# A two-layer graph network: a shorter bank count in the layer-0 sums, deviations by chunks in the first stage, one-hots three windows ahead in the one-head sums

## What is computed

```python
xn = _layernorm(x)
x = x + gnn0(xn, edges) + mix0(xn)       # 8 heads of 32, edge features in the score
x = x + ffn0(_layernorm(x))              # 8 experts
xn = _layernorm(x)
x = x + gnn1(xn, edges) + mix1(xn)       # 4 heads of 128, then 1 head of 256
x = x + ffn1(_layernorm(x))              # 32 experts

# in each graph step, per head:
ex    = jnp.exp(alpha - segment_max(alpha, dst)[dst])
attn  = ex / segment_sum(ex, dst)[dst]
out   = segment_sum(h[src] * attn[..., None], dst)
```

## Time and profile before

| | us |
|---|---|
| three runs | 3051.1, 3053.57, 3061.77 |
| median | 3053.57 |
| the profiled execution | 3050.74 |
| its span, first to last instruction | 3049.0 |
| PE busy | 2105.7 (69%) |
| DVE busy | 2085.5 (68%) |
| POOL busy | 1440.7 (47%) |
| ACT busy | 827.2 (27%) |

### The profile page before, as it was taken

The page is one execution under the profiler, slowest core; times in us unless marked ns, Lnnn a source line. Parts: engine busy times, 40 slices in busy tenths (PEclk is TensorE's granted clock), DMA queues, the critical chain, the costliest instruction groups (busy, mean ns, idle before and its releaser), DMA issues. The chain is left out here.

```text
span 3049.0 us, 51563 instructions
## 1 busy us (share of the span) xinstructions
PE 2105.7 (69%) x11892; PEld 1580.5 (52%) x11893; DVE 2085.5 (68%) x4524; ACT 827.2 (27%) x2459; POOL 1440.7 (47%) x1486
## 2 busy tenths in 40 slices
PE   2634878757887389948665499999756188887372
PEld 2322434445665355624565377787645177776252
DVE  7496888888888343353478688888677277778442
ACT  2314444431001212124200467676500000001110
POOL 2477777700000310130553777777357677771234
PEclk9866998979998599979777699999856599998586
DMA  4777999935775278843997788898589645550085
GB/s 151 208 205 218 269 269 270 271 139 172 229 232 149 98 256 271 271 125 118 340 393 263 238 278 281 277 287 275 137 285 269 190 130 158 159 148 20 35 257 175
DMA packets 447837, 649.13 MB, mean 213 GB/s; under 512 B 67552, under 2 KB 328286, under 8 KB 447123
## 3 DMA queue, kind: packets, MB, share of 16 engines
q1 hardware_dynamic: 329747, 351.62, 37.0%
q0 software_dynamic: 82640, 248.85, 27.6%
q10 hardware_dynamic: 35296, 46.90, 4.5%
HBM read 478.83 MB, written 169.68 MB: 213 GB/s over the span
## 5 line engine op out<-in xcount | busy, mean ns | idle before, releaser
L1616 POOL DMA_INDIRECT wide<-table,src_col x264 | 277.9, 1053 | 80.7 <-issue 73.3
L1777 PE MATMUL sum_h_ps<-wide,sum_h_hot 128*128 x880 | 254.1, 412 | 75.4 <-DVE wide L1802 45.6
L1037 POOL DMA_INDIRECT arena_b<-table,al x272 | 258.1, 949 | 89.2 <-issue 85.2
L1753 POOL DMA_INDIRECT wide<-table,al x262 | 257.9, 984 | 85.8 <-issue 58.8
L1659 PE MATMUL sum_h_ps<-wide,sum_h_hot 128*128 128x261 f32 x1056 | 253.4, 389 | 37.2 <-ACT wide L1644 21.2
L1885 PE MATMUL sum_ps<-wide,sum_hot 128*128 128x264 f32 x880 | 211.9, 394 | 52.4 <-DVE sum_hot L1895 27.5
L1659 PEld LDWEIGHTS sum_h_ps<-wide,sum_h_hot 128*128 128x128 f32 x1056 | 197.3, 191 | 85.2 <-issue 29.7
L1173 POOL DMA_INDIRECT wide<-table,src_col x132 | 138.6, 1050 | 198.1 <-issue 134.1
L1885 PEld LDWEIGHTS sum_ps<-wide,sum_hot 128*128 128x128 f32 x880 | 163.8, 191 | 100.4 <-issue 74.9
L1058 PE MATMUL score_ps_hd<-wide,score_hot 128*128 x1320 | 209.5, 301 | 0.0
L1777 PEld LDWEIGHTS sum_h_ps<-wide,sum_h_hot 128*128 128x128 f32 x880 | 155.2, 197 | 92.8 <-issue 79.7
(11 more groups left out here) (537 smaller groups left out, 4991.9 us busy)
## 6 DMA issues: line engine op xcount, KB each, us to landing
wide<-edge_h SPq DMA_DIRECT2D x220, 264.0 KB, 3.0
edge_h<-arena_b SPq DMA_DIRECT2D x68, 528.0 KB
arena_b<-kept SPq DMA_DIRECT2D x66, 516.0 KB, 5.2
wide<-edge_rows SPq DMA_DIRECT2D x110, 256.0 KB, 4.7
score_h_hot<-hots SPq DMA_DIRECT2D x220, 128.0 KB
kept<-wide ACTq DMA_DIRECT2D x40, 516.0 KB, 8.5
wide<-kept SPq DMA_DIRECT2D x65, 257.0 KB
wide<-in_f_w SPq DMA_DIRECT2D x16, 1024.0 KB, 10.0
```

What stands on the lines that cost most here:

```text
L1037: pool.indirect_dma_start(rows[:, q, k, :], None, K.table0[:, :], bass.IndirectOffsetOnAxis(ap=K.src_blk[:, g * GS + k:g * GS + k + 1], ax ...
L1616: pool.indirect_dma_start(rows[w][:, s, 0:RW], None, table, bass.IndirectOffsetOnAxis(ap=K.src_col[:, w * SUB + s:w * SUB + s + 1], axis=0 ...
L1753: pool.indirect_dma_start(ring[:, b % RING, s, :], None, table, bass.IndirectOffsetOnAxis(ap=K.src_blk[:, b * SUB + s:b * SUB + s + 1], ax ...
L1777: pe.matmul(ps[:, u, 0:RW], lhsT=hot[:, q, s, :], rhs=ring[:, bass.ds(places[j % 4], 1), s, :].rearrange("p a r -> p (a r)"), start=(s == ...
```

## The change

There are three edits in three stages.

In the layer-0 sums PE no longer reads four counts of freed banks, but one, that of the fourth window of the group, and waits for it once, ahead of the group's first window. Tiles are met in order, so the fourth window's count is the largest of the four.

In the one-head sums `AHEAD` goes from 2 to 3: DVE makes three windows' one-hots before the loop, and in the loop those of window w + 3 ahead of the addition of window w.

In the first stage ACT takes the square root by chunks (`deviations`), the first ahead of all normalizations and each later one at the third tile of the chunk before it; DVE's inversions go between the chunks' moments, the last two behind the last moments. SP stores the first three chunks of the table ahead of the keys, the other two behind the clips; the parts of the attributes go half by SP and half by ACT at its end; PE's transposes of the edge columns go from tiles 6 and 15 to tile 17 and to the end. The lines of the later stages move by 20 (L1885 becomes L1905).

```diff
@@ first stage, SP @@
+            for c in range(3):
+                store_table(c)
             sp.wait_ge(s_gather, 16 * 5 * WC)
             sp.wait_ge(s_key, 1)
...
+            for c in range(3, NT // U):
+                store_table(c)
             sp.wait_ge(s_key, 3)
...
             sp.wait_ge(s_parts, 6)
-            for k in range(ENC_ROWS // 3):
-                sp.dma_start(K.attr_parts[k].rearrange("(c p e) -> p c e", c=WC, p=WP), attr_parts[:, :, k, :]).then_inc(s_stored, 16)
-            sp.wait_ge(s_one, 1)
-            for c in range(NT // U):
...
+            for k in range(0, ENC_ROWS // 3, 2):
+                store_part(sp, k)
@@ first stage, ACT @@
+            def deviations(c):
+                part = slice(c * U, (c + 1) * U)
+                act.wait_ge(s_var, c + 1)
+                act.activation(T["std"][:, part], T["var"][:, part], ACT.Sqrt, bias=K.eps[:, 0:1]).then_inc(s_std, 1)
+
             def norm(t):
+                if t % U == 2 and t + U < NT:
+                    deviations(t // U + 1)
+                if t % U == 0:
+                    act.wait_ge(s_rstd, t // U + 1)
...
-            act.wait_ge(s_var, NT // U)
-            act.activation(T["std"][:, :], T["var"][:, :], ACT.Sqrt, bias=K.eps[:, 0:1]).then_inc(s_std, NT // U)
-            act.wait_ge(s_rstd, NT // U)
+            deviations(0)
...
             out(NT - 1)
+            act.wait_ge(s_parts, 6)
+            for k in range(1, ENC_ROWS // 3, 2):
+                store_part(act, k)
@@ first stage, DVE @@
             for c in range(NT // U):
                 chunk_moments(dve, step, K, T, c, s_var)
-            for c in range(NT // U):
-                chunk_invert(dve, step, T, c, s_std, s_rstd)
+                if c != 1:
+                    chunk_invert(dve, step, T, max(0, c - 1), s_std, s_rstd)
+            chunk_invert(dve, step, T, NT // U - 1, s_std, s_rstd)
@@ first stage, PE @@
-                if t == 6:
+                if t == 17:
                     turn(0, src_f)
                     turn(1, rel)
-                if t == 15:
-                    pe.wait_ge(s_blkout, 1)
-                    turn(2, last)
             project(NT - 1)
+            pe.wait_ge(s_blkout, 1)
+            turn(2, last)
@@ one-head sums @@
-        J, QH, U2, QS, QG, AHEAD = 20, 5, 4, 4, 8, 2
+        J, QH, U2, QS, QG, AHEAD = 20, 5, 4, 4, 8, 3
@@ layer-0 sums, PE @@
                     if j % 4 == 0:
-                        needs = load_four(pe, K.bank[0:1, 0, bass.ds(w, 4)], 1, NT)
                         banks = load_four(pe, K.bank[0:1, 1, bass.ds(w, 4)], 0, BANKS - 1)
+                        need = pe.value_load(K.bank[0:1, 0, bass.ds(w + 3, 1)], min_val=1, max_val=NT)
+                        pe.wait_ge(s_free, need)
                     pe.wait_ge(s_hot, w + 1)
                     pe.wait_ge(s_msg, w + 1)
-                    pe.wait_ge(s_free, needs[j % 4])
```

More of the change, by code:

```diff
@@ L300, in items_project_l0, with store_part @@
         key_flat = K.key_flat
+        def store_part(queue, k):
+            queue.dma_start(K.attr_parts[k].rearrange("(c p e) -> p c e", c=WC, p=WP), attr_parts[:, :, k, :]).then_inc(s_stored, 16)
         block = st.block()
@@ L318, in _, with store_table @@
             sp.dma_start(key_flat[1 + WS * P:2 + WS * P].unsqueeze(0), guard[:, :]).then_inc(s_shift, 16)
+            sp.wait_ge(s_one, 1)
+            def store_table(c):
+                t = slice(c * U, (c + 1) * U)
+                out = K.table0[c * U * P:(c + 1) * U * P, :].rearrange("(t p) r -> p t r", p=P)
+                sp.wait_ge(s_adout, (c + 1) * U)
+                sp.dma_start(out[:, :, ROW0:ROW0 + H0], K.att_n[:, t, 0:H0]).then_inc(s_table, 16)
+                sp.wait_ge(s_hout, (c + 1) * U)
+                sp.dma_start(out[:, :, 0:ROW0], K.tab0[:, t, :]).then_inc(s_table, 16)
+            for c in range(3):
+                store_table(c)
             sp.wait_ge(s_gather, 16 * 5 * WC)
```

## The result

The changed kernel takes 2994.05 us (median of four runs, 2990.41 to 2998.77), the kernel before 3052.34 in the same comparison: a ratio of 0.9827, interval 0.9801 to 0.9853. That is 58 us less; 60 were forecast, and 2991. The profiled execution of the changed kernel is the slowest of its four runs; its span is 2997.1 us against 3049.0.

A forecast was written before the change was run, and what follows sets the result against it. No engine bounds the whole, a row of stages between barriers; PE's sequencer bounds the layer-0 sums. Terms -33 - 26 - 1.5 = -60.5 on 3050.74 us give 2990.2, stated as 2991; range 2982 to 3017.

The forecast's parts named there:

- 3.25 + 4 x 0.33 = 4.6 us: Layer-0 sums: PE's register loading plus four window issues equals the group's period, so PE's sequencer is the bound.
- The rival that the sequencer would not get faster: Layer-0 sums: single load and wait cost as much as the removed load; 3024 us, at half 3007; chance 0.09.
- the pitch of 1.02: Layer-0 sums: us per window after the change, taken between SP's 1.01 and DVE's 1.03; term -33 us.
- priced at 0.55 us: Layer-0 sums: cost of PE's new single load, taken from the same operation in the one-head sums.
- The forecast's reading of the 600 ns: Layer-0 sums: the skill's tensor_load floor differs from the trace's 0.33 us a load, and the trace decides.
- the 4.1 us a group: Layer-0 sums: sequencer time by the 600 ns floor, 3.6 + 2 x 0.27, level with DVE; term a few us smaller.
- a term mis-sized: One-head sums: PE closes up to the gathers and ends with them, 2765.2 against 2791.5; term -26 us.
- the mean pitch that I used, 336.5 / 262 = 1.284, holds such cases already: One-head sums: gather pitch in us, said to include gathers slowed by DVE already; an argument against longer gathers.
- the first rival: One-head sums: gathers take time back as busier DVE meets more; at 1.05 us each, 26 us, 3017; chance 0.13.
- One sign of being wrong: One-head sums: the prediction is wrong if the gathers' median leaves 0.95.
- The cause as I put it: One-head sums: busier DVE meets more gathers, whose descriptors can't be written during its operations that take both ports.
- The row of 1.14 us in the earlier trace: Single gathers in DVE's dense stretches took 1.14 us against a median of 0.947; said to agree with the port lock.

The follow-up runs named there:

- the experiment with columns: Changed kernel, but DVE makes the one-head sums' second one-hot matrix by two operations of one matrix operand and a column, not one of two matrix operands: 2997.21 us.
- both gains together: Changed kernel with the second one-hots by two operations of one matrix operand and the first stage's square roots early: 2981.72 us, ratio 0.9762 to the kernel before.

## Why the prediction was right, and where not

**Layer-0 sums: right, in mechanism and size.** That PE's own sequencer was the bound was read from the sum 3.25 + 4 x 0.33 = 4.6 us, against the profile's own naming of DVE. The single load alone brings it, and the four counts loaded with one wait bring none. The rival that the sequencer would not get faster is refuted, and so is any weight on the three waits: without them, but with all loads, the stage took 270.1 us. That a further load saved gives nothing shows that the bound has gone on, to DVE, as the pitch of 1.02 assumed (1.025 measured). The single load was priced at 0.55 us and took some 0.75; it cost nothing, since the sequencer no longer sets the pace. The forecast's reading of the 600 ns in the Trainium skill's "DMA: Bandwidth & Descriptors", section "Latency and other measured facts", stands: the loads took 0.33 us each in the earlier trace rows, so the measurement decides. That the gap went doesn't tell, since the 4.1 us a group that the forecast estimated by that figure are what a group now takes anyway.

**One-head sums: right in mechanism, a term mis-sized.** The step was "the mean pitch that I used, 336.5 / 262 = 1.284, holds such cases already". PE's distance behind the gathers fell by the forecast 26.0 us, but the pitch went to 344.2 / 262 = 1.314: 7.7 us. This is the first rival, at a quarter to a third of the size that it was given; it was priced from the median of 0.947, though the mean was 0.984 already. One sign of being wrong that the forecast named came true with it: the gathers' median left 0.95 in this profile (0.982). It is a poor sign, since a second profile of the same kernel has a median of 0.950 with the same long mean, 1.010.

The cause as I put it (DVE, busier, meets more gathers, by operations that take both ports) is only half right. The row of 1.14 us in the earlier trace rows doesn't say which operation held that gather. DVE's row does, a comparison of two SBUF operands that started 0.10 us ahead of it:

```profile
2599.38 0.42 DVE L1793 TENSOR_TENSOR sum_h_one<-iota_row,rel_col 128x256 f32<-128x256 f32 x1
```

The count and the experiment with columns show that this one operation makes nearly all of the loss, and that twice as many operations with one operand make far less. That more gathers fall on it with a third window ahead is counted (152 for 94, and 85 for 30 at the same place, 0.15 to 0.20 us behind its start). Why they do is argued, not shown: the wait of PE for counted landings ties DVE's windows to POOL's rhythm, so that hits repeat.

**First stage: right within 1 us, in a small sum of large parts.** The first normalization came at 41.80 (near 42 was forecast), DVE 10.7 us late (12), the end at 101.1 (101.1 to 102.9). That the late DVE is a loss is shown by the roots taken early: another 7 us.

**The sum.** 60.5 us were forecast, and the three stages lost 53.1 in the profiled executions; the 7.7 of the gathers are the difference. That the median, 2994, still lies only 3 from 2991 is in part luck. The medians are 58 apart, the two profiled executions 52: 2998.77 is 8.6 above the 2990.2 that the sum gave for that execution, and it lies 4.7 above the median of its kernel, the one before 1.6 below. Stages that the change doesn't touch scatter by as much: the four-head sums took 432.0 us in the profiled execution before, 440.1 after, and between 433.7 and 439.1 in the profiles of the other kernels, with either number of windows ahead. One pair of profiles can't tell 8 us there.

## What to carry to other kernels

Where PE idles by the same amount in every group of windows, add up its sequencer's own records before believing the engine that the profile names: register loads and issues that sum to the period are the bound; here taking out one load gave 32 us, and taking out three waits gave nothing. When a consumer is freed to follow gathers on GpSimd closely, look at which VectorE operations beside them read two operands from SBUF; writing one of them with a column operand gave 6.5 us here (10.0 in the profiles of both gains together), at the price of a longer DVE window. A square root or any other small step that two engines pass to and fro should be put as early as its input allows, not just ahead of its use, when one of the two has other work queued behind it.

## What was not expected of the hardware

A gather's 0.95 us on POOL grew to 1.11 and 1.14 us when it started just behind the start of DVE's 0.42 us comparison of two SBUF operands, and in the kernel after to 1.22 at 0.02 us behind that start and to 1.39 in one gather that started 0.15 us ahead of it. It stayed within 0.942 to 0.955 us when it started while DVE added a PSUM operand or was idle, and reached 1.06 under the one-column comparisons of the kernel that has them. A four-number load into PE's registers takes 1.6 us, of which the memory's part is 0.33; the rest is register arithmetic and range checks on the sequencer, one after the other.
